# Three attention stages: score products in two row halves, far distance term in the operands, VectorE on the near half only, zero spans left out

## The chip, the core and the metric

One Trainium2 chip, of which the program uses one core. A core has TensorE (PE in the profile; PEld is its weight load), VectorE (DVE), ScalarE (ACT), GpSimd (POOL) and SyncE (SP, which here only issues DMAs). The matrix results lie in PSUM, everything else that the engines touch in SBUF. The metric is the device time of one execution in microseconds, median of several runs.

## What is computed

A block of eight layers over `x` of shape (4, 1024, 128): attention a, a mixture of experts, attention b, the same mixture of experts again, a fast-weights layer, a LoRA layer, attention c and the LoRA layer again. Each takes a layer norm of `x` first. Only the three attentions are touched. They have 16 heads of 8 dimensions, 4 batches and 1024 tokens:

```python
# a: distance term added to the scores
scores = jnp.einsum('bqhd,bkhd->bhqk', q, k) / math.sqrt(head_dim)
bias = -jnp.abs(pos[None, :] - pos[:, None])
scores = scores + slopes[None, :, None, None] * bias[None, None]   # slopes[h] = 0.7071 ** h
probs = jax.nn.softmax(scores, axis=-1)
...
# b: scores multiplied by a distance factor
scores = jnp.einsum('bhsd,bhtd->bhst', q, k) / jnp.sqrt(D)
decay = jnp.exp(-jnp.abs(distance_decay[0]) * dist)
attn = jax.nn.softmax(scores * decay, axis=-1)
...
# c: no distance term, heads centred over the tokens
corr = jax.nn.softmax(jnp.einsum('bthd,bThd->bhtT', x_centered, x_centered), axis=-1)
```

## The kernel before

The eight layers run one after the other, each in its own blocks; the block of one step starts when all engines have left the one before. Every engine has its own instruction stream, and semaphores tie them. The order is written out by hand, so nothing is planned by a tool.

An attention layer is: `layer_norm` (L77; with it POOL clears the operand buffers, `Operands.clear`, L336), `project_qkv` (L189; c has `centre_and_split` in its place), for a and b `bound_scores` and a branch (`choose`, L983) that takes the fast form when a bound on the scores is below a limit, then `attend_transposed` (L623), `normalise` and `project_out`.

`project_qkv` makes q and k in 16 units of 128 features x 512 tokens (w = 0 is q, w = 1 is k). To keep float32 accuracy in bf16 products each number is split into three bf16 parts: DVE adds the bias (L257), ACT casts the first part (L298), DVE takes the rest (L266), ACT casts the second part (L304), POOL makes the third (L311), and SP stores the three parts into `parts_dram` (L319). ACT also squares (L301) for the bound.

`attend_transposed` works on 16 groups, one for four heads (GH = 4) of one batch. The operands of a score product are six combinations of the parts, 8 rows each, so 48 of the 128 rows of PE are in use; the others hold zeros (c has one more row, at 64, with the shift). A group has 32 units: eight blocks J of 128 keys by four heads j. The steps of a unit:

- `scores` (L702 to L716): two products c = 0, 1 of 128 keys x 512 queries into a slot of `s_ps`; there are three slots (SLOTS), and the wait at L709 or L711 is for the slot's last reader.
- in b, DVE multiplies the 1024 scores by a slice of the distance table and writes `probs` in SBUF (L836); in a it does slope x distance + score (L838) for the heads j = 1, 2, 3. ACT then takes the exponential in place (L779). In a the head j = 0 goes another way: ACT takes the exponential from PSUM (L775), and POOL multiplies by a factor table (L694). In c ACT reads the scores straight from PSUM (L786).
- `sum_up` (L718 to L732): per J and half c, four float32 products with `v_cols` (one per head, each in its own 32 columns of PE) add to `o_ps`. It waits for the exponential of the block's last head.

PE's order is fixed in `pair` (L734): the products of unit n + 3, then, at n % 4 = 3 and n % 4 = 1, one half's sums. After a group the sums are copied to `out_t`: by ACT in a and b (`take_sums`, L762, after its second unit of the next group), by DVE in c (L820). The loads of a group's operands (L672, 12 DMAs of 64 KB; L675 in c) are issued by SP into one of two buffers when the sums of the group before last have been taken. The DVE loop runs over head groups and then batches, as do all others.

## Time and profile before

| | us |
|---|---|
| median of three runs | 3812.92 |
| range of the runs | 3808.32 to 3816.82 |
| span of the profiled execution | 3812.1 |
| PE busy in it | 3231.4 (85%) |
| DVE busy | 2548.2 (67%) |
| ACT busy | 2544.1 (67%) |
| POOL busy | 721.3 (19%) |
| first to last start of a score product: a | 562.8 |
| the same, b | 596.1 |
| the same, c | 516.4 |

The three attention loops together are 1675 us of the span, 44%. The shares of busy time over the whole span are averages over layers with different limits, so each stage has to be read by itself. The spans of the matmuls are modelled at their ends: the start times say more than the busy time. The chain that ended last covers only the last layer, since the layers are kept apart by blocks.

### The profile page before, as it was taken

Reading aid. Unit: us, or ns where it says so; the run is one execution under the profiler, and the core shown is the slowest. Engines: PE = TensorE matmul, PEld = TensorE weight load, DVE = VectorE, ACT = ScalarE, POOL = GpSimd, SP = SyncE. Lnnn points to the kernel's source line nnn. Section 1 sums busy time; section 2 is a strip of 40 time slices with the busy share of each in tenths; the row PEclk is TensorE's granted clock in tenths of the full one; section 3 lists DMA queues with packets and bytes.
Section 4 is the critical chain, followed back from the end, with each engine's and each line's share of the span. In section 5 each row is a group of like instructions: output and inputs, shape, how many; then the busy total and the mean of one; then the engine's idle time right before and its main releaser. Section 6 shows DMA issues by size and latency. Waiting matters only on the chain. (4 is left out here: it accounts for less than half of the span.)

```text
span 3812.1 us, 55628 instructions
## 1 busy us (share of the span) xinstructions
PE 3231.4 (85%) x18220; PEld 1431.3 (38%) x18220; DVE 2548.2 (67%) x3577; ACT 2544.1 (67%) x3503; POOL 721.3 (19%) x395
## 2 busy tenths in 40 slices
PE   3899999799996688888889999788878367999987
PEld 2122222567764211111257766522356341222235
DVE  6788888677777699999967777577799551000022
ACT  5899999455444699999845545555433347999971
POOL 4455555000002200000000000165544010000010
PEclk8999999899998899999989999899989558999995
DMA  3111110000000211111000000000000001111100
GB/s 97 30 18 24 25 21 13 23 0 1 0 0 5 84 25 17 25 17 25 9 23 0 1 0 0 24 1 0 0 0 0 2 22 39 25 25 25 25 11 23
DMA packets 47299, 66.97 MB, mean 18 GB/s; under 512 B 6993, under 2 KB 25297, under 8 KB 46545
## 3 DMA queue, kind: packets, MB, share of 16 engines
q1 hardware_dynamic: 47184, 65.54, 8.2%
q8 instruction: 60, 0.98, 0.1%
q14 instruction: 55, 0.44, 0.0%
HBM read 47.56 MB, written 17.96 MB: 17 GB/s over the span
## 5 line engine op out<-in xcount | busy, mean ns | idle before, releaser
L836 DVE TENSOR_TENSOR b_direct_probs<-b_direct_s_ps,b_distance 128x1024 f32<-128x1024 f32 x512 | 583.4, 1212 | 30.4 <-PE b_direct_s_ps L713 16.7
L779 ACT ACTIVATE b_direct_probs<-b_direct_probs 128x1024 f32<-128x1024 f32 x512 | 534.7, 1057 | 74.1 <-DVE b_direct_probs L836 45.2
L838 DVE SCALAR_TENSOR_TENSOR a_direct_probs<-a_distance,a_slopes,a_direct_s_ps 128x1024 f32<-128x1024 f32 x384 | 470.3, 1277 | 111.4 <-PE a_direct_s_ps L713 111.4
L1353 ACT ACTIVATE m_mix_hidden<-m_mix_up_ps 128x512 f32<-128x512 f32 x512 | 305.7, 597 | 295.3 <-PE m_mix_up_ps L1297 295.3
L786 ACT ACTIVATE c_att_probs<-c_att_s_ps 128x1024 f32<-128x1024 f32 x512 | 482.5, 1029 | 13.7 <-PE c_att_o_ps L728 13.1
L1305 PE MATMUL m_mix_down_ps<-m_w,m_mix_hidden 128*128 128x128 f32 x4096 | 474.8, 276 | 0.0
L1305 PEld LDWEIGHTS m_mix_down_ps<-m_w,m_mix_hidden 128*128 128x128 f32 x4096 | 467.2, 192 | 15.3 <-issue 15.3
L1297 PE MATMUL m_mix_up_ps<-m_mix_ZT,m_w 128*128 128x512 f32 x1024 | 471.6, 619 | 0.0
L779 ACT ACTIVATE a_direct_probs<-a_direct_probs 128x1024 f32<-128x1024 f32 x384 | 400.4, 1057 | 36.2 <-DVE a_direct_probs L838 12.5
L820 DVE COPY c_out_t<-c_att_o_ps 128x512 f32 x32 | 20.6, 686 | 515.1 <-PE c_att_o_ps L728 515.1
L694 POOL TENSOR_TENSOR a_direct_probs<-a_direct_probs,a_XN 128x1024 f32<-128x1024 f32 x128 | 304.4, 2379 | 266.7 <-ACT a_direct_probs L775 266.7
L728 PE MATMUL b_direct_o_ps<-b_direct_probs,b_v_cols 128*32 128x512 f32 x2048 | 269.4, 604 | 59.1 <-ACT b_direct_probs L779 59.0
L713 PE MATMUL b_direct_s_ps<-b_q_rows,b_k_rows 128*128 128x512 bf16 x1024 | 277.2, 386 | 37.0 <-DVE b_direct_probs L836 18.6
L713 PE MATMUL c_att_s_ps<-c_q_rows,c_k_rows 128*128 128x512 bf16 x1024 | 271.1, 385 | 43.2 <-DMA c_q_rows<-shift 31.5
L728 PE MATMUL a_direct_o_ps<-a_direct_probs,a_v_cols 128*32 128x512 f32 x2048 | 269.4, 604 | 37.9 <-ACT a_direct_probs L779 28.3
L713 PE MATMUL a_direct_s_ps<-a_q_rows,a_k_rows 128*128 128x512 bf16 x1024 | 270.3, 384 | 32.7 <-DMA a_k_rows<-qk_parts 18.2
L728 PE MATMUL c_att_o_ps<-c_att_probs,c_v_cols 128*32 128x512 f32 x2048 | 269.5, 604 | 0.4 <-ACT c_att_probs L786 0.4
L1297 PEld LDWEIGHTS m_mix_up_ps<-m_mix_ZT,m_w 128*128 128x128 f32 x1024 | 157.4, 190 | 291.1 <-ACT m_mix_hidden L1353 274.1
L1458 DVE TENSOR_REDUCE m_mix_mixed<-m_mix_weighted 128x128 f32<-128x1024 f32 x128 | 246.8, 1928 | 4.4
L1273 POOL TENSOR_TENSOR X<-X,m_Z x16 | 22.0, 1376 | 985.1 <-DVE m_Z L1462 985.1
L713 PEld LDWEIGHTS c_att_s_ps<-c_q_rows,c_k_rows 128*128 128x128 bf16 x1024 | 78.1, 98 | 318.9 <-ACT c_att_probs L786 233.6
L1669 POOL TENSOR_TENSOR f_recur_dots_prods<-f_recur_dots_vecs 128x512 f32<-128x512 f32 (+1 forms) x64 | 173.0, 2715 | 104.2 <-DVE f_recur_dots_vecs L1701 104.2
(330 smaller groups left out, 3982.7 us busy)
## 6 DMA issues: line engine op xcount, KB each, us to landing
qk_parts<-a_qkv_parts SPq DMA_DIRECT2D x16, 384.0 KB, 2.5
a_q_rows<-qk_parts SPq DMA_DIRECT2D x96, 64.0 KB
a_k_rows<-qk_parts SPq DMA_DIRECT2D x96, 64.0 KB
qk_parts<-b_qkv_parts SPq DMA_DIRECT2D x16, 384.0 KB, 2.5
b_q_rows<-qk_parts SPq DMA_DIRECT2D x96, 64.0 KB
b_k_rows<-qk_parts SPq DMA_DIRECT2D x96, 64.0 KB
c_q_rows<-qk_parts SPq DMA_DIRECT2D x96, 64.0 KB
c_k_rows<-qk_parts SPq DMA_DIRECT2D x96, 64.0 KB
```

The costliest lines, as they stand in the source:

```text
L694: pool.tensor_tensor(first, first, factor[:, at:at + SEQ], ALU.mult).then_inc(damped, 1)
L713: last = pe.matmul(s_ps[:, n % SLOTS, c * BANK:(c + 1) * BANK], k_rows[:, half, j, J * P:(J + 1) * P], q_rows[:, half, j, c * BANK:(c + 1) ...
L728: last = pe.matmul(o_ps[VW * j:VW * (j + 1), c, :], v_cols[:, half, J, j, :], probs[:, J % 2, j, c * BANK:(c + 1) * BANK], start=(J == 0), ...
L779: act.activation(out, out, ACT.Exp).then_inc(exped, 1)
L786: act.activation(out, s_ps[:, n % SLOTS, :], ACT.Exp).then_inc(exped, 1)
L836: ins = dve.tensor_tensor(out, scores_, near, ALU.mult)
L838: ins = dve.scalar_tensor_tensor(out=out, in0=near, scalar=slopes[:, bass.ds(hg * GH + j, 1)], in1=scores_, op0=ALU.mult, op1=ALU.add)
L1297: pe.matmul(up_ps[:, f % UP_BANKS, :], w["w1"][:, f * P:(f + 1) * P], ZT[:, half, :], start=True, stop=True).then_inc(up_done, 1)
L1305: last = pe.matmul(down_ps[:, t % 2, e, :], hidden[:, e * HALVES + h, t * P:(t + 1) * P], w["w2"][:, e * HALVES + h, :], start=(h == 0), s ...
L1353: act.activation(hidden[:, f, :], up_ps[:, f % UP_BANKS, :], ACT.Silu).then_inc(silu_done, 1)
L1458: dve.tensor_reduce(mixed[:, :], weighted[:, :, :].rearrange("p e d -> p d e"), AX, ALU.add).then_inc(summed, 1)
L1669: return engine.tensor_tensor(prods[:, c % 2, at:at + n, :], vecs[:, c % 2, 0:n, :], vecs[:, c % 2, other:other + 1, :].to_broadcast([P, n ...
```

## The change

1. **Two row halves.** The 48 operand rows stand twice, at rows 0 to 47 and 64 to 111 (`PAIR_ROW = 64`). The two products of a unit take 64 rows each, one the upper and one the lower half, in place of 128 rows each. SP issues 24 loads a group in place of 12; in c the query rows are half as long each, and one shift row goes to each half.
2. **Near and far.** Of a unit's 1024 queries, the 512 on the side on which its keys lie are near, the others far. For the far side the distance splits into a key's distance to the middle and a query's, so that its term can be put into the operands: in a six more rows with the products of slope x distance (`BiasRows`, made by POOL in the layer norm and stored in `bias_dram`; two more loads a group), in b a second, damped version of q and k (`damp`), which doubles the split and the store in `project_qkv` (16 units, now 32 splits). DVE works only on the near side, in place in PSUM, for all four heads.
3. **ACT from PSUM in all three.** The exponential reads `s_ps` and writes `probs`. A slot is free when ACT has read it, where before it was free when DVE had. The factor table, POOL's product and the ACT copies of the sums are gone; DVE takes the sums, after its third unit of the next group.
4. **Zero spans.** In a `alibi_span` leaves out queries so far from the keys that the exponential is zero: for head h beyond ceil(152 / slope). Widths are 280 to 942 of 1024 for the first four heads (mean 556.1; the near part 433.8), 736 to 1024 for the next four (mean 991.8), full for the rest. Sums over a left-out edge are cut in two pieces.
5. **Loops.** Batches outside, head groups inside and written out; an exponential ahead of the loop (`warm`). `clear` writes the rows of ones only in c, in two stretches of 32 rows. The limit of the branch in a is 24 in place of 30.

```diff
@@ project_qkv
+            def take(x):
+                u, v = divmod(x, VERS)
...
+                if v == 0:
+                    dve.wait_ge(projected, u + 1)
+                    dve.tensor_scalar(full[:, b, :], qk_ps[:, u % RING, :], b_qk[:, w:w + 1],
+                                      scale if w == 0 else 1.0, ALU.add, ALU.mult).then_inc(biased, 1)
+                else:
...
+                    dve.tensor_tensor(full[:, b, :], full[:, (x - 1) % RING, :], damp[:, at:at + CHUNK],
+                                      ALU.mult).then_inc(biased, 1)
@@ attend_transposed
+            def scores(hg, n, b):
...
+                at = hg * UNITS + n
+                back = at - SLOTS if at >= SLOTS else max(m for m in range(-SLOTS, 0) if slot(0, m + NB) == slot(0, at))
+                pe.wait_ge(exped, b * NB + (back + 1 + SLOTS))
                 for c in range(2):
-                    last = pe.matmul(s_ps[:, n % SLOTS, c * BANK:(c + 1) * BANK],
-                                     k_rows[:, half, j, J * P:(J + 1) * P],
-                                     q_rows[:, half, j, c * BANK:(c + 1) * BANK], start=True, stop=True)
+                    if not part(hg * GH + j, J, c):
+                        continue
+                    left, right = part(hg * GH + j, J, c)
+                    tile = int(c != J // (JT // 2)) if by_dve else c
+                    rows = slice(PAIR_ROW * tile, PAIR_ROW * (tile + 1))
+                    last = pe.matmul(s_ps[:, slot(hg, n), left:right], k_rows[rows, half, j, J * P:(J + 1) * P],
+                                     q_rows[rows, half, j, left:right], start=True, stop=True)
                 last.then_inc(scored, 1)
...
+                        act.activation(probs[:, J % 2, j, lo:hi], s_ps[:, slot(hg, n), lo:hi], ACT.Exp).then_inc(exped, 1)
...
+                if slopes is None:
+                    ins = dve.tensor_tensor(held, held, near, ALU.mult)
+                else:
+                    h = hg * GH + j
+                    ins = dve.scalar_tensor_tensor(out=held, in0=near, scalar=slopes[:, h:h + 1], in1=held,
+                                                   op0=ALU.mult, op1=ALU.add)
...
+                    for n in range(UNITS):
+                        adjust(b, hg, n)
+                        if n == SLOTS - 1:
+                            if hg:
+                                take_sums(b, hg - 1)
@@ alibi_attention
+def alibi_span(h, J):
+
+
+    reach = math.ceil((UNDERFLOW + 2 * SAFE_BAND_SCORE) / alibi_slopes()[h])
+    return max(0, J * P - reach), min(SEQ, (J + 1) * P + reach)
```

The copies of the sums change their engine. ACT's stream in b before, at the start of a group inside its loop (L779 is the exponential, L766 the copy; the other rows keep registers):

```order
L779 ACTIVATE b_direct_probs<-b_direct_probs 128x1024
L778 REGISTER_ALU
L779 ACTIVATE b_direct_probs<-b_direct_probs 128x1024
L763 ISA
L766 ISA
L766 COPY b_out_t<-b_direct_o_ps 128x512
L766 ISA
L766 COPY b_out_t<-b_direct_o_ps 128x512
L778 REGISTER_ALU
```

DVE's stream in b now, over the first batch (L828 is the product on the near half, now in place in `s_ps`; L817 the copy of a group's sums):

```order
L828 TENSOR_TENSOR b_direct_s_ps<-b_direct_s_ps,b_distance 128x512 x35
L817 COPY b_out_t<-b_direct_o_ps 128x512 x2
L828 TENSOR_TENSOR b_direct_s_ps<-b_direct_s_ps,b_distance 128x512 x32
L817 COPY b_out_t<-b_direct_o_ps 128x512 x2
L828 TENSOR_TENSOR b_direct_s_ps<-b_direct_s_ps,b_distance 128x512 x32
L817 COPY b_out_t<-b_direct_o_ps 128x512 x2
L828 TENSOR_TENSOR b_direct_s_ps<-b_direct_s_ps,b_distance 128x512 x29
```

The two copies stood behind ACT's second unit and stand behind DVE's third unit of the next group; 32 adjustments lie between two pairs.

In `project_qkv` of b DVE's stream is now, for the units four and five (L262 is the bias, L267 the damping product, L276 the rest, L285 the bias of v):

```order
L262 TENSOR_SCALAR b_qkv_full<-b_qkv_qk_ps,b_b_qk 128x512
L276 TENSOR_TENSOR b_qkv_rest<-b_qkv_full,b_qkv_parts 128x512
L285 TENSOR_TENSOR b_V<-b_qkv_v_ps,b_b_v 128x512
L267 TENSOR_TENSOR b_qkv_full<-b_qkv_full,b_damp 128x512
L276 TENSOR_TENSOR b_qkv_rest<-b_qkv_full,b_qkv_parts 128x512
L262 TENSOR_SCALAR b_qkv_full<-b_qkv_qk_ps,b_b_qk 128x512
L276 TENSOR_TENSOR b_qkv_rest<-b_qkv_full,b_qkv_parts 128x512
```

Where a unit had one bias and one rest, it now has a damping product and a second rest as well.

PE's stream in a now, in the first head group (L741 score products, L760 sums):

```order
L741 MATMUL a_direct_s_ps<-a_q_rows,a_k_rows 128x512
L741 MATMUL a_direct_s_ps<-a_q_rows,a_k_rows 128x48
L748 ISA
L749 ISA
L760 MATMUL a_direct_o_ps<-a_direct_probs,a_v_cols 32x280
L760 MATMUL a_direct_o_ps<-a_direct_probs,a_v_cols 32x343
L760 MATMUL a_direct_o_ps<-a_direct_probs,a_v_cols 32x432
L760 MATMUL a_direct_o_ps<-a_direct_probs,a_v_cols 32x512
```

Every product there was 512 wide; now each is as wide as its head's span.

## Rows read from the trace of the kernel before

**Rows 1.** Groups by line: busy us, mean ns of one, idle before and releaser.

```profile
L836 DVE TENSOR_TENSOR b_direct_probs<-b_direct_s_ps,b_distance 128x1024 f32<-128x1024 f32 x512 | 583.4, 1212 | 30.4 <-PE b_direct_s_ps L713 16.7 <-PE b_direct_o_ps L728 12.5
L838 DVE SCALAR_TENSOR_TENSOR a_direct_probs<-a_distance,a_slopes,a_direct_s_ps 128x1024 f32<-128x1024 f32 x384 | 470.3, 1277 | 111.4 <-PE a_direct_s_ps L713 111.4
L779 ACT ACTIVATE b_direct_probs<-b_direct_probs 128x1024 f32<-128x1024 f32 x512 | 534.7, 1057 | 74.1 <-DVE b_direct_probs L836 45.2
L786 ACT ACTIVATE c_att_probs<-c_att_s_ps 128x1024 f32<-128x1024 f32 x512 | 482.5, 1029 | 13.7 <-PE c_att_o_ps L728 13.1
L1353 ACT ACTIVATE m_mix_hidden<-m_mix_up_ps 128x512 f32<-128x512 f32 x512 | 305.7, 597 | 295.3 <-PE m_mix_up_ps L1297 295.3
L786 ACT ACT_TABLE_LOAD x16 | 20.5, 1283 | 24.2 <-PE c_att_s_ps L713 23.9
```

**Rows 2.** Timeline of c, two half steps: start us, length us, instructions, idle before.

```profile
3312.06 1.04 PE L713 MATMUL c_att_s_ps<-c_q_rows,c_k_rows 128*128 128x512 bf16 x4
3312.19 3.77 ACT L786 ACTIVATE c_att_probs<-c_att_s_ps 128x1024 f32<-128x1024 f32 x4 [0.16 <-PE c_att_o_ps L728]
3313.02 1.07 PE L728 MATMUL c_att_o_ps<-c_att_probs,c_v_cols 128*32 128x512 f32 x8
3314.02 1.04 PE L713 MATMUL c_att_s_ps<-c_q_rows,c_k_rows 128*128 128x512 bf16 x4
```

**Rows 3.** Timeline of b at the end of a group.

```profile
1413.93 1.92 PE L728 MATMUL b_direct_o_ps<-b_direct_probs,b_v_cols 128*32 128x512 f32 x16
```

**Rows 4.** Timeline of c: the copies of a group's sums by DVE.

```profile
3303.15 1.29 DVE L820 COPY c_out_t<-c_att_o_ps 128x512 f32 x2 [30.99 <-PE c_att_o_ps L728]
```

**Rows 5.** Groups by line: DVE products of 128x512.

```profile
L2039 DVE TENSOR_TENSOR X<-X,l_y_ps 128x512 f32<-128x512 f32 x16 | 11.0, 687 | 85.6 <-PE l_y_ps L2005 85.6
L1701 DVE SCALAR_TENSOR_TENSOR f_recur_dots_vecs<-f_recur_dots_vec_ps,f_recur_dots_low 128x512 f32<-128x512 f32 x128 | 85.3, 683 | 71.6 <-ACT f_recur_dots_low L1659 71.1
```

**Rows 6.** Timeline: the first loads of a, and the first score product.

```profile
90.96 3.08 SPq L672 DMA_DIRECT2D a_q_rows<-qk_parts  x6
94.28 2.44 SPq L672 DMA_DIRECT2D a_k_rows<-qk_parts  x6
102.69 0.61 PE L713 MATMUL a_direct_s_ps<-a_q_rows,a_k_rows 128*128 128x512 bf16 x1 [18.18 <-DMA a_k_rows<-qk_parts]
```

**Rows 7.** Stretches: us, busy us of the engines, granted clock, DMA share, GB/s.

```profile
3340.00:3342.00 2.00, 2.00 (x20) 0.47 (x12) 0.00 (x0) 1.98 (x3) 0.00 (x0) 1.00 0.53 79
```

**Rows 8.** Groups by line: DVE in the projection of b.

```profile
L266 DVE TENSOR_TENSOR b_qkv_rest<-b_qkv_full,b_qkv_parts 128x512 f32<-128x512 f32 x16 | 14.3, 893 | 0.7 <-ACT b_qkv_parts L298 0.7
L257 DVE TENSOR_SCALAR b_qkv_full<-b_qkv_qk_ps,b_b_qk 128x512 f32<-128x512 f32 x16 | 11.8, 740 | 11.9 <-PE b_qkv_qk_ps L242 11.9
```

**Rows 9.** Timeline of c's layer norm: POOL clears, DVE normalises.

```profile
3104.21 6.92 POOL L341 MEMSET c_k_rows<- 1x8192 bf16 x1
3104.24 8.57 DVE L112 TENSOR_SCALAR c_XN<-X,c_ln_neg_mean,c_ln_rstd 128x128 f32<-128x128 f32 x8
3114.28 2.14 DVE L112 TENSOR_SCALAR c_XN<-X,c_ln_neg_mean,c_ln_rstd 128x128 f32<-128x128 f32 x8
```

**Rows 10.** Groups by line: POOL's product of 128x1024, in a.

```profile
L694 POOL TENSOR_TENSOR a_direct_probs<-a_direct_probs,a_XN 128x1024 f32<-128x1024 f32 x128 | 304.4, 2379 | 266.7 <-ACT a_direct_probs L775 266.7
```

**Rows 11.** PE stretches with alternating row counts (last layer), and one plain.

```profile
3751.59 0.79 PE L2005 MATMUL l_y_ps<-l_lora_b,l_outer_t 64*128 64x128 f32 x2
3752.31 0.79 PE L2003 MATMUL l_y_ps<-l_lora,l_XT 128*128 128x128 f32 x2
2947.30 3.63 PE L1795 MATMUL f_recur_values_y_ps<-f_out,f_recur_values_mixed_t 128*128 128x128 f32 x16 [1.10 <-ACT f_recur_values_mixed_t L1828]
```

**Rows 12.** Stretches with the granted clock (seventh figure).

```profile
1300.00:1600.00 300.00, 260.85 (x1523) 55.83 (x1524) 291.58 (x256) 273.01 (x270) 2.82 (x7) 0.99 0.13 21
2953.00:2960.00 7.00, 5.04 (x41) 4.62 (x42) 4.15 (x5) 1.01 (x1) 0.00 (x0) 1.00 0.00 0
3750.00:3800.00 50.00, 50.00 (x154) 35.04 (x152) 9.02 (x14) 4.64 (x8) 0.00 (x0) 0.50 0.00 0
```

More of the change, by code:

```diff
@@ L812, in _ @@
+            with act.Fori(0, BATCH) as b:
+                batch(b)
         @block.vector
@@ new lines, in batch @@
+            def batch(b, first):
+                for hg in range(HG):
+                    if not by_dve:
+                        take_sums(b, hg)
+                        continue
+                    for n in range(UNITS):
+                        adjust(b, hg, n)
+                        if n == SLOTS - 1:
+                            if hg:
+                                take_sums(b, hg - 1)
+                            elif not first:
+                                take_sums(b - 1, HG - 1)
```

436 lines of the change are left out of this document (231 added, 205 removed).

## Prediction

> **What bounds the kernel now.** The totals come first and say little: three busy engines over stages with different limits. So I read the groups by line, then the timeline inside each attention loop. In **b** VectorE is the bound: its 512 products of 1212 ns with 30.4 us of idle time are 614 us of the stage, ScalarE has 74.1 us of idle time, most of it for DVE [rows 1]. In **a** DVE has only three heads of four (470.3 us plus 111.4 idle), and POOL's 128 products of 2379 ns form a second chain beside it [rows 1, 10]. In **c** DVE has no product. There TensorE sets the pace: a half step of two units is 1.96 us from one start of products to the next (3312.06 to 3314.02), of which 0.96 are four products and 1.00 the sums; a block J is 3.92 us. ACT's four exponentials take 3.77 us of it and wait 0.16 [rows 2]. The 482.5 us over 512 are 0.942 us of ACT a unit (the single record, 1029 ns, overlaps its neighbour) [rows 1].
>
> **What the change makes of it.** Row halves, near halves and the reading from PSUM leave ACT as the only engine with 0.942 us of work a unit in all three stages: DVE's product of 128x512 takes 0.683 to 0.687 us [rows 5], and PE must fall below 3.77 us a block.
>
> *PE.* Today 8 products of 0.24 us and two sums phases make 3.92 us [rows 2]. If the two halves run side by side, a unit costs one product time: 4 x 0.24 + 2 x 1.00 = 2.96 us, with four more switches of geometry 3.3. That the array can work on separate parts at once, rows 2 show for columns only: eight records of sums (four float32 products) take 1.07 us, though one alone must stream its 512 columns several times. That it does so for rows nothing here shows. Side by side costs 0 against the ACT bound; one after the other leaves 3.92 us or more. I take side by side, since the two halves read other rows, other weights and another PSUM bank each. The Trainium skill, "TensorE: Matmul & The Clock Gate", Part 3: Packing small matmuls, states a measured 3.07 times for four row tiles, and that weight loads overlap only between different row groups; by it this step holds, and no row here can check it.
>
> *The slot chain.* A slot now waits for: end of its exponential, 0.05, the products 0.24 to 0.4, DVE 0.69, 0.05: about 1.2 us. With three slots it has 2 x 0.942 = 1.88 us. A sums phase of 1.00 us in front of the products [rows 2] costs at most the rest of the slack, 0.7. So no wait inside a group.
>
> *The end of a group, a and b.* DVE now takes the sums, after its third product of the next group. Let the last exponential end at T. PE runs the next products and both halves' sums of the last block, 0.41 + 1.92 [rows 3], then 0.17, DVE's two copies, 1.29 [rows 4]: T + 3.8. Only then comes the adjustment of the fourth unit, 0.69: T + 4.5. ACT has three units ready and would want it at T + 2.83. Stall: 1.7 us a group; its cover is those three units. Between 0.5 (PE splits its sums sooner) and 2.5. In c no adjustment is behind the copies: none.
>
> - **b**: 32 x 0.942 = 30.15, + 1.7 = 31.85 a group, x 16 = 509.5, minus 3 for the tail that "first to last start" leaves out: 506.5 against 596.1: **-90**.
> - **c**: 16 x 30.15 - 3 = 480 against 516.4: **-36**. The 16 table loads (20.5 us, [rows 1]) lie in that gain: ACT has one left.
> - **a**: ACT costs 0.844 us per 1000 columns ((1029 - 597) / 512, [rows 1]) plus 0.078 a unit so that 1024 give 0.942. Widths of 991.8 give 0.915: 29.3 + 1.7 = 31.0 for the second head group; the third and fourth 31.85 each. In the first, mean width 556.1, ACT needs 0.547 a unit, 17.5 a group. But there the cover is gone: a block of four units is 2.2 us of ACT and PE's two sums phases alone are near 2. Each phase delays the slot chain; I add 0.55 us to half the units: 17.5 + 8.8 + 1.7 = 28.0. Bounds: 19.2 (all hidden) and 31.85 (no gain at all). Four batches: 4 x (28.0 + 31.0 + 2 x 31.85) = 491, minus 3 = 488 against 562.8: **-75**, bounds -110 and -59. Cutting the first group's sums in pieces adds PE instructions, not columns. POOL leaves the loop; where its chain stood [rows 10], DVE's fourth head stands at 0.69.
>
> *Loads.* SP issues 24 or 26 a group in place of 12. Inside a loop they have the time from T + 3.8 to the end of the next group, 24 to 28 us; 12 took 11.7 us from first issue to use (90.96 to 102.69, [rows 6]), twice that is 23.5: hidden, with nothing to spare in a's first group. Nor does a transfer slow PE: 3340 to 3342 has DMA at 0.53 and a PE that issues as in rows 2 [rows 7]. But the first group of a stage has no cover: its 12 more loads stand in SP's queue ahead of the first product. 12 issues took 5.8 us (rows 6: 3.08 + 2.44 and the gap), 12 loads wholly 11.7; between these +8.5 a stage, **+25** for three (18 to 35).
>
> *Projection of b.* Each of 16 units gets one more product (0.69) and one more rest (0.69 to 0.89, [rows 5, 8]) on DVE, which had 11.9 us idle over the 16 [rows 8]: 1.4 each, **+22** (12 to 30). ACT, POOL and SP get a second split too, but less than DVE in sum.
>
> *Layer norms.* In a, POOL's BiasRows are some 16 short and 8 row-long operations on 1024 elements; a memset of one partition and 8192 took 6.92 [rows 9], and goes. DVE beside a busy POOL took 8.57 us for eight normalisations that took 2.14 without [rows 9]. **+8** for a (2 to 14); **-5** for b (the memset goes, two iotas and one exponential come); **+7** for c (a second memset of 6.92). Sum +10.
>
> Sum: -90 - 36 - 75 + 25 + 22 + 10 = **-144** against the execution's own 3812.1, so 3668; the median of the runs is 0.8 higher: **3669 us**.
>
> **Rivals.**
> *Row halves one after the other.* The block on PE is then 3.92 us plus what b's and a's group ends add: c keeps its 516 (+36), b and the last three head groups of a lose 0.15 to 0.25 us a block (+31 and +23): 3669 + 90 = 3759. For it: no row shows rows in parallel. Against: other banks, other rows.
> *Switches and queues.* PE changes geometry four times a block more often than it would with whole-array products. In the last layer, where products of 64 and 128 rows alternate, one starts every 0.36 x 2 = 0.72 us, while a run of 8 equal ones (16 records) takes 3.63, 0.454 each [rows 11]: 0.27 us a switch at the low clock, perhaps half at the high one. On the 3.3 us block that is up to 0.5 more, 3.8: ACT waits now and then, most in a's first head group. With steady loads that no longer fit, +18 in a, +9 in b, +4 in c at least: 3700 to 3760. The Trainium skill, "TensorEngine Tiling (Array Packing)", Key Properties, says that changing the mode drains the engine; by it this is the likelier direction of error, and rows 11 agree with a cost of 0.27 us.
> *Less than forecast is lost*: the first head group at its floor and group ends nearly hidden, below 3640.
> *Slower: the granted clock.* The change leaves PE with gaps: some 3 of 3.77 us busy. The records show 0.99 in b's loop with PE busy 87% and 1.00 at 5.04 of 7 us, but also 0.50 at 100% busy in the alternating stretch of the last layer, where the rows in use change like here [rows 12]. If the loops were granted 0.5 (1.2 GHz), a block would be about 1.9 + 2 x 2.0 + switches = 6.2 us in place of 3.77: +2.4 x 128 = +310 us a stage. One stage at that clock gives 3980, all three about 4550. It turns the result at 144 / 930, 16% of the attention time.
> *The change doesn't do what it says*: the fast form is left if the bound in a exceeds 24; over the given inputs the longest q times the longest k is 13, so it is taken.
>
> **How the numbers follow.** Forecast 0.65; row halves serial 0.10; switches and queues 0.11; below 3640 0.08; clock 0.04; elsewhere within 0.2% 0.01, slower for a cause not named 0.01. The measurement tells 0.2%, about 8 us, from no change. Faster 0.94, same 0.01, slower 0.05. The forecast's own bounds (stalls -1.2 to +0.8 a group, the first head group -35 to +15, loads -7 to +10, projection -10 to +8) rarely fall together: 3635 to 3700. Half of the two PE rivals has to be within, so the range is 3630 to 3745.
>
> **What would show it.** Right: in c ACT busy with no idle time before L786's successor, unit pace 0.94, pairs of products with one start; in b and a one gap of 1 to 2.5 us a group on ACT, released by DVE, right behind the two copies. First product of a stage some 8 us later after the first load. Granted clock 1.00. Wrong: pairs with starts 0.216 us apart; ACT released by PE inside a group of b or c; SP's loads the last releaser at a group's start; a clock of 0.5 in any loop; the first head group of a at over 30 us.

## The result and the profile after

The changed kernel takes 3771.95 us (median of four runs, 3769.95 to 3773.79) against 3813.69: ratio 0.989, 95% interval 0.9876 to 0.9904. It is faster by 1.1%, as forecast in its direction, but by 42 us instead of 144, and lies outside the range (3630 to 3745). The profiled execution has a span of 3772.1 us against 3812.1.

Where the 40 us of the two profiled executions come from (a loop is counted from the first to the last start of a score product, and the stretches between the loops):

| us | before | after | change | forecast |
|---|---|---|---|---|
| loop of a | 562.8 | 550.8 | -12 | -75 |
| loop of b | 596.1 | 516.1 | -80 | -90 |
| loop of c | 516.4 | 472.0 | -44 | -36 |
| first load of a stage to its first product (a, b, c) | 11.7, 10.9, 11.5 | 28.6, 27.2, 19.6 | +41 | +25 |
| projection of b, first bias to last rest | 32.9 | 69.2 | +36 | +22 |
| layer norms, the rest | | | +19 | +10 |

The large miss is a's loop, the next two are the first loads and b's projection. The page's groups, line, out<-in, count | busy, mean ns of one | idle before and what ended it, show that ACT reads PSUM everywhere and where it waits:

```profile
L804 ACT ACTIVATE a_direct_probs<-a_direct_s_ps 128x1024 f32<-128x1024 f32 (+10 forms) x512 | 432.5, 939 | 148.6 <-DVE a_direct_s_ps L831 111.4
L804 ACT ACTIVATE b_direct_probs<-b_direct_s_ps 128x1024 f32<-128x1024 f32 x512 | 474.8, 1092 | 71.6 <-DVE b_direct_s_ps L828 63.9
L804 ACT ACTIVATE c_att_probs<-c_att_s_ps 128x1024 f32<-128x1024 f32 x512 | 470.2, 1166 | 22.5 <-PE c_att_s_ps L741 19.5
L828 DVE TENSOR_TENSOR b_direct_s_ps<-b_direct_s_ps,b_distance 128x512 f32<-128x512 f32 x512 | 333.6, 695 | 181.5 <-PE b_direct_s_ps L741 181.4
```

Beside [rows 1]: DVE has 181.5 us of idle time in b instead of 30.4, and is no longer the bound. ACT is busy for 0.918 us a unit in c (470.2 / 512), a little less than the 0.942 that PE had set. In a, though, ACT has 148.6 us of idle time.

**c and the inside of a group went as forecast.** The timeline of c after (start us, length us), beside [rows 2]:

```profile
3312.04 1.07 PE L760 MATMUL c_att_o_ps<-c_att_probs,c_v_cols 128*32 128x512 f32 x8
3313.04 0.91 PE L741 MATMUL c_att_s_ps<-c_q_rows,c_k_rows 64*128 64x512 bf16 x4
3313.88 1.06 PE L760 MATMUL c_att_o_ps<-c_att_probs,c_v_cols 128*32 128x512 f32 x8
3314.87 0.91 PE L741 MATMUL c_att_s_ps<-c_q_rows,c_k_rows 64*128 64x512 bf16 x4
```

Two units take 1.83 us instead of 1.96, and the pace is now ACT's. A pair of 64-row products has one start (3 ns apart in the records), where the 128-row products before stood 226 ns apart, so the two row halves do run side by side. The Trainium skill, "TensorE: Matmul & The Clock Gate", Part 3: Packing small matmuls, has products on different rows of the array run at the same time, and the trace agrees.

**The end of a group in b** (timeline) is the stall that the prediction worked out:

```profile
1562.74 1.92 PE L760 MATMUL b_direct_o_ps<-b_direct_probs,b_v_cols 128*32 128x512 f32 x16
1564.60 0.96 PE L741 MATMUL b_direct_s_ps<-b_q_rows,b_k_rows 64*128 64x512 bf16 x6
1564.86 1.29 DVE L817 COPY b_out_t<-b_direct_o_ps 128x512 f32 x2 [1.23 <-PE b_direct_o_ps L760]
1566.07 1.89 DVE L828 TENSOR_TENSOR b_direct_s_ps<-b_direct_s_ps,b_distance 128x512 f32<-128x512 f32 x3
1566.80 23.94 ACT L804 ACTIVATE b_direct_probs<-b_direct_s_ps 128x1024 f32<-128x1024 f32 x26 [1.68 <-DVE b_direct_s_ps L828]
```

Both halves' sums, two copies, then the adjustment, and ACT resumes after 1.68 us (1.9 in the mean over b's groups); 1.7 was forecast. Behind it ACT runs 26 exponentials without a gap.

**The loads** are what the prediction had too cheap. First the timeline at the start of a: first and last issue of the first group's 26 loads and the first product, then the stretch of 28 us and, for comparison, 2 us of the first group's loads in the kernel before (us, busy us of PE, PEld, DVE, ACT, POOL, granted clock, DMA share, GB/s):

```profile
97.00 0.40 SPq L697 DMA_DIRECT2D a_k_rows<-qk_parts  x1
...
107.00 0.29 SPq L712 DMA_DIRECT2D a_k_rows<-bias_rows  x1
...
125.64 1.05 PE L741 MATMUL a_direct_s_ps<-a_q_rows,a_k_rows 64*128 64x280 bf16 x3 [34.61 <-DMA a_k_rows<-bias_rows]
```

```profile
97.00:125.00 28.00, 0.00 (x0) 0.00 (x0) 0.00 (x0) 0.61 (x2) 0.71 (x2) 0.50 0.52 67
```

```profile
98.00:100.00 2.00, 0.00 (x0) 0.00 (x0) 0.00 (x0) 0.00 (x0) 0.00 (x0) 0.50 0.55 83
```

All 26 are issued in 10 us, but land 18.6 us after the last issue. The DMA share stands at 0.52 all the while, with nothing else to load: of the 16 DMA engines' time half is used, and between 102 and 120 us the trace has never fewer than 8 packets in flight and mostly 8. The share was the same before. But the loads have become slower too: 67 GB/s in place of some 83, and a packet of 2 KB takes 251 ns in the mean where it took 185. In half_loads below, with 14 loads, it is 247 ns, so the number of loads is not the reason; what is, stays open. The same holds inside the loop. The loads for a's third group, and that group's start (timeline):

```profile
158.86 0.29 SPq L697 DMA_DIRECT2D a_k_rows<-qk_parts  x1
...
187.76 0.61 PE L741 MATMUL a_direct_s_ps<-a_q_rows,a_k_rows 64*128 64x512 bf16 x2 [3.75 <-DMA a_k_rows<-bias_rows]
...
190.31 1.02 ACT L804 ACTIVATE a_direct_probs<-a_direct_s_ps 128x1024 f32<-128x1024 f32 x1 [4.43 <-PE a_direct_o_ps L760]
```

28.9 us again from the first issue to the use, and PE stands 3.75 us for it, with ACT behind. The waits of a's loop (engine, what it waited for: us in total, times, longest) say how often:

```profile
PE a_direct_s_ps L741 <- DMA a_k_rows<-bias_rows: 65.7, 13, 34.6
```

34.6 of this is the start of the stage; 31 us are the starts of twelve groups. And the clock (stretches of the three loops, granted clock the third figure from the end), beside 1.00, 1.00 and 0.99 of the same stretches before:

```profile
125.60:677.00 551.40, 455.78 (x3132) 112.02 (x3136) 371.67 (x542) 430.76 (x511) 5.63 (x14) 0.88 0.36 46
1367.00:1884.00 517.00, 444.99 (x3056) 89.07 (x3056) 351.55 (x542) 473.39 (x511) 5.63 (x14) 0.96 0.36 46
3170.70:3643.00 472.30, 432.74 (x3048) 89.04 (x3048) 19.33 (x30) 468.13 (x511) 5.64 (x14) 0.99 0.27 38
```

In a PE was granted half the clock (1.2 GHz) for 130 us of the loop, before the change for 5. That time is twice what the granted clock lacks to 1, times the stretch: 2 x 0.118 x 551.

### The profile page after: what moved, and what is told of

It is laid out like the page before. It is cut to its first block and busy times, and to the rows that moved or that the text cites. A ratio compares the mean times of both kernels' runs of the same rounds, so it can differ in the third digit from the quotient of the medians.

```text
span 3772.1 us, 56220 instructions
## 1 busy us (share of the span) xinstructions
PE 3041.1 (81%) x18300; PEld 1382.0 (37%) x18300; DVE 2266.9 (60%) x3801; ACT 2361.2 (63%) x3456; POOL 452.0 (12%) x310
## 5 line engine op out<-in xcount | busy, mean ns | idle before, releaser
L804 ACT ACTIVATE a_direct_probs<-a_direct_s_ps 128x1024 f32<-128x1024 f32 (+10 forms) x512 | 432.5, 939 | 148.6 <-DVE a_direct_s_ps L831 111.4
L804 ACT ACTIVATE b_direct_probs<-b_direct_s_ps 128x1024 f32<-128x1024 f32 x512 | 474.8, 1092 | 71.6 <-DVE b_direct_s_ps L828 63.9
L804 ACT ACTIVATE c_att_probs<-c_att_s_ps 128x1024 f32<-128x1024 f32 x512 | 470.2, 1166 | 22.5 <-PE c_att_s_ps L741 19.5
L831 DVE SCALAR_TENSOR_TENSOR a_direct_s_ps<-a_distance,a_slopes,a_direct_s_ps 128x512 f32<-128x512 f32 (+3 forms) x512 | 354.1, 732 | 195.2 <-PE a_direct_s_ps L741 194.1
L828 DVE TENSOR_TENSOR b_direct_s_ps<-b_direct_s_ps,b_distance 128x512 f32<-128x512 f32 x512 | 333.6, 695 | 181.5 <-PE b_direct_s_ps L741 181.4
L817 DVE COPY c_out_t<-c_att_o_ps 128x512 f32 x32 | 20.6, 686 | 479.1 <-PE c_att_o_ps L760 479.1
L741 PE MATMUL a_direct_s_ps<-a_q_rows,a_k_rows 64*128 64x512 bf16 (+12 forms) x984 | 201.3, 400 | 130.2 <-DMA a_k_rows<-bias_rows 65.7
L760 PE MATMUL a_direct_o_ps<-a_direct_probs,a_v_cols 128*32 128x512 f32 (+14 forms) x2168 | 289.9, 592 | 1.0 <-ACT a_direct_probs L804 1.0
L741 PE MATMUL b_direct_s_ps<-b_q_rows,b_k_rows 64*128 64x512 bf16 x1024 | 199.8, 402 | 103.7 <-ACT b_direct_probs L804 39.8
L760 PE MATMUL b_direct_o_ps<-b_direct_probs,b_v_cols 128*32 128x512 f32 x2048 | 280.1, 625 | 2.3 <-ACT b_direct_probs L804 2.3
L760 PE MATMUL c_att_o_ps<-c_att_probs,c_v_cols 128*32 128x512 f32 x2048 | 271.2, 607 | 1.0 <-ACT c_att_probs L804 1.0
L741 PE MATMUL c_att_s_ps<-c_q_rows,c_k_rows 64*128 64x512 bf16 x1024 | 197.4, 390 | 78.7 <-DMA c_q_rows<-shift 39.2
L741 PEld LDWEIGHTS b_direct_s_ps<-b_q_rows,b_k_rows 64*128 64x128 bf16 x1024 | 47.0, 93 | 387.7 <-ACT b_direct_probs L804 339.7
L741 PEld LDWEIGHTS a_direct_s_ps<-a_q_rows,a_k_rows 64*128 64x128 bf16 x984 | 45.9, 95 | 376.5 <-ACT a_direct_probs L804 287.1
L741 PEld LDWEIGHTS c_att_s_ps<-c_q_rows,c_k_rows 64*128 64x128 bf16 x1024 | 47.6, 93 | 358.7 <-ACT c_att_probs L804 315.2
```

The costliest lines, as they stand in the source:

```text
L741: last = pe.matmul(s_ps[:, slot(hg, n), left:right], k_rows[rows, half, j, J * P:(J + 1) * P], q_rows[rows, half, j, left:right], start=Tr ...
L760: last = pe.matmul(o_ps[VW * j:VW * (j + 1), c, lo - c * BANK:hi - c * BANK], v_cols[:, hg % 2, J, j, :], probs[:, J % 2, j, lo:hi], start ...
L804: act.activation(probs[:, J % 2, j, lo:hi], s_ps[:, slot(hg, n), lo:hi], ACT.Exp).then_inc(exped, 1)
L828: ins = dve.tensor_tensor(held, held, near, ALU.mult)
L831: ins = dve.scalar_tensor_tensor(out=held, in0=near, scalar=slopes[:, h:h + 1], in1=held, op0=ALU.mult, op1=ALU.add)
```

## The experiments

Theory A: the doubled loads bound a's groups and the start of every stage, because they use only half of the DMA engines, and the low clock in a follows largely from these waits. Theory B: PE's gaps and its geometry switches inside the loop cost the time. The names of the kernels are those of the table. Each kernel below is the changed kernel with one edit unless it says otherwise. The loops of all of them (first to last start of a score product) follow. a's loop is the same code and the same loads in the changed kernel, damp_psum and no_damp, and takes 551, 555 and 564 us: that much it varies from one execution to another, so differences of a's loop below some 13 us prove nothing by themselves.

| kernel | median us | a | b | c | us at half clock in a, b, c |
|---|---|---|---|---|---|
| before | 3814 | 562.8 | 596.1 | 516.4 | 5, 5, 8 |
| changed | 3772 | 550.8 | 516.1 | 472.0 | 130, 46, 10 |
| half_loads | 3679 | 497.8 | 509.8 | 471.7 | 60, 31, 9 |
| pool_sem | 3705 | 499.5 | 511.2 | 471.1 | 67, 36, 8 |
| full_spans | 3781 | 564.6 | 519.6 | 471.0 | 105, 44, 7 |
| pool_full | 3709 | 505.5 | 510.4 | 471.1 | 27, 38, 8 |
| serial_rows | 4330 | 780.1 | 811.1 | 532.3 | 595, 610, 61 |
| rows128 | 3770 | 528.1 | 540.7 | 506.3 | 25, 6, 4 |
| rows64 | 4300 | 794.1 | 860.9 | 531.9 | 644, 721, 60 |
| damp_psum | 3761 | 554.5 | 516.1 | 470.9 | 134, 51, 7 |
| no_damp | 3744 | 564.1 | 517.5 | 473.0 | 120, 49, 8 |
| split_sums | 3766 | 558.8 | 509.0 | 471.1 | 106, 34, 8 |
| all3 | 3657 | 476.6 | 498.2 | 471.1 | 25, 28, 8 |

Three expectations below use 140 us of half clock for a's loop in the changed kernel and 605 for serial_rows; 130 and 595 are right. No conclusion hangs on the difference.

### Half of the loads left out

```
-        LOADS = 4 * len(Q_PARTS) + 2 * (bias_dram is not None or shift_dram is not None)
+        LOADS = 2 * len(Q_PARTS) + 2 * (bias_dram is not None) + (shift_dram is not None)
...
-                    for tile in range(2):
+                    for tile in range(1):
```

> The changed kernel, all three attentions without the loads of rows 64 to 111 (the second copy of the operands; those rows hold zeros, so one half of the scores is without its product; a keeps its two loads of bias rows, c one shift row). Same work on PE, DVE and ACT, 12 to 14 loads a group in place of 24 to 26. In the changed kernel's trace the first product of a waits 28.6 us from the first issue, c and b likewise, and a's groups begin 2.6 to 3.5 us late. Theory A, the loads are the bound of a and the start of every stage, and the low clock of a comes from PE's idle time at the group starts: first products some 14, 13 and 9 us after the first issue, -13 in a and b each and -6 in c; a's groups fall from 34.5 to about 32 (the first head group to 28), -45; stretches at clock 0.5 in a's loop fall from 140 us to under 50. In all 3772 - 32 - 45 - up to 15 = 3680 to 3695. Theory B, PE's gaps and geometry switches inside the loop cost the time and the clock: only the starts move, 3740, and 0.5 stands in a for over 100 us as before.

3679.25 us (two runs), 93 less. The stages start 11, 13 and 10 us sooner (the stretch before each loop), a's loop loses 53 us and b's 6. The waits of a's loop for loads are the stage's start alone:

```profile
PE a_direct_s_ps L741 <- DMA a_k_rows<-bias_rows: 22.8, 1, 22.8
```

The time at half clock in a falls by more than half (130 to 60 us, where theory A had under 50). Theory A holds, theory B's 3740 does not. PE and DVE run the same instructions in both kernels, so the clock's fall in a is to that extent the loads' doing, unless the zeros in half of the rows have a part in it; the next kernel has the real operands. Of the 53 us, 31 are the waits themselves; that the other 22 are products and sums at half clock is argued, not separated, and 13 of them lie within what a's loop varies.

### The second half's loads issued by POOL

```
-        loaded = [k.sem(f"{tag}_loaded{half}") for half in range(2)]
+        loaded_sp = [k.sem(f"{tag}_loaded{half}") for half in range(2)]
+        loaded_pool = [k.sem(f"{tag}_pooled{half}") for half in range(2)]
...
+        def load(eng, b, hg, tile):
+            loaded = (loaded_sp, loaded_pool)[tile]
...
+                    load(sp, b, hg, 0)
...
+                    load(pool, b, hg, 1)
```

> The changed kernel, with the loads of the second row half issued by POOL with a semaphore of their own; same bytes, same result. While a group's 26 loads run, the DMA share of the changed kernel stands at 0.5 and 8 packets are in flight. Theory A, the loads are bound by the DMA engines that SP's queue uses for this shape, and POOL's queue uses others too: as fast as without the second half's loads (3679), 3675 to 3700, with a's loop near 505 and DMA share above 0.5 at a stage's start. Theory C, the limit is that of the shape whoever issues: no change, 3765 to 3780, or slower by POOL's own cost of issuing, up to +20.

3705.22 us, ratio 0.9715 to before (0.9699 to 0.9731), with the same bytes and the same result. a's loop is 499.5, as with half of the loads, none of its group starts waits, and it has 67 us at half clock, so the zeros of half_loads were not what kept the clock up. Theory A holds and theory C's 3765 to 3780 does not. The profiled execution (span 3692.3) lies 17 us above that of half_loads (3675.0), 5 of them at the start of a and 8 ahead of c, where the stage starts keep a part of the price. The other three runs took 3704 to 3707, and the median is a little over the expected 3700; no trace shows why they are longer than the profiled one. The stretch at the start of a, first of this kernel, then of the changed one:

```profile
97.00:107.00 10.00, 0.00 (x0) 0.00 (x0) 0.00 (x0) 0.07 (x1) 9.18 (x17) 0.50 0.80 104
```

```profile
97.00:107.00 10.00, 0.00 (x0) 0.00 (x0) 0.00 (x0) 0.61 (x2) 0.71 (x2) 0.50 0.48 67
```

The same shape of load from two issuers has a DMA share of 0.80 and 104 GB/s, from one 0.48 and 67; the 26 loads take 23.2 us (96.4 to 119.6) instead of 28.6. So what held SP's loads of 8 partitions at half is not a limit of the shape whoever issues. The Trainium skill, "DMA: Bandwidth & Descriptors", Why a DMA increments its semaphore by 16 and not by 1, says that a transfer runs on the largest number up to 16 that divides both outermost dimensions, for SP's queue always the lowest-numbered ones, for POOL's from a cursor that moves on; by it an 8-partition load takes 8, and the traces agree: 8 packets in flight and a share of 0.5. That POOL's loads gained because they ran on other engines is the page's reading; no run here tells it from a limit of SP's queue. I had not weighed that rule.

### Full spans in a, with SP's loads and with POOL's

```
-                                      slopes=slopes, bias_dram=bias_dram, span=alibi_span)
+                                      slopes=slopes, bias_dram=bias_dram)
```

> The changed kernel with full spans in a: the first two head groups compute all 1024 queries of each unit. Theory A, a's groups are bound by their 26 loads (about 28.6 us from issue to landing, plus 4 to 5 us from the group's start to the issue), whatever ACT has to do: a's loop stays at 552 within 12 us, 3765 to 3785. Rival: the narrow spans save what ACT's widths say, 11 to 14 us a batch for the first head group and 1 for the second, so leaving them out costs 45 to 60, 3820.

> The kernel of pool_sem with full spans in a. With SP's loads, full spans cost 9 us (3781 against 3772), since a's groups were bound by their loads. Theory A: with the loads no longer the bound, the spans' worth shows: the first head group goes from 30.3 us to the 32.0 to 33.5 of the others, the second from 30.5 to 31.1: 4 x 3 = +12, up to +16 with the widths of ACT's floor: 3717 to 3722. The forecast for the change had put the first head group at 28.0 against 31.85, 15 us. Rival, the spans are worth nothing or even cost since PE is the bound there in either form: 3700 to 3706.

3781.37 with SP's loads, 9 us more than the changed kernel, in theory A's interval: the part of the change that leaves work out was worth little while loads bound the groups. 3709.01 with POOL's, 4 us more than pool_sem (two runs, 3706.28 and 3711.75, against 3694.03 to 3706.76): no difference that can be told. Here theory A's 3717 to 3722 fell, and the rival's 3700 to 3706 is the nearer one. The first head group averages 30.3 us a group in pool_sem with narrow spans and 30.9 with full ones in pool_full, since with short exponentials ACT is no longer what is late there: a block of four units still has PE's two sums phases, at half clock in part (67 us of a's loop at half clock with narrow spans, 50 of them in the four groups of the first head group; 27 and 16 with full spans). So the zero spans leave out two fifths of ACT's work in a quarter of a's groups (17.5 us of 30.15 remain) and return nothing that can be measured in this form.

### Both products on the same 64 rows

```
-                    rows = slice(PAIR_ROW * tile, PAIR_ROW * (tile + 1))
+                    rows = slice(0, PAIR_ROW)
```

> The changed kernel with both products of a unit on rows 0 to 63 (the second half's rows are loaded and not used, so a and b lack the far side's distance term). Theory A, two row halves run side by side and this is what c gained from: pairs start 0.216 us apart, c's block of four units goes from 3.67 to 3.9 us or more, c's loop from 473 to about 510; b's groups from 32.2 to about 34, +28; a, bound by its loads, by 0 to 15. In all 3835 to 3850. Rival: the pairs gain nothing that counts, c's gain came from something else (the table loads, the loop order): c within 5 us, 3772.

4330.38 us, ratio 1.1355 (1.1207 to 1.1503). Both theories missed by 480 us or more: c stayed within 25 us (532 against 510, its first group at half clock), a and b stood at half clock for some 600 us each (its loops of a and b):

```profile
124.30:905.00 780.70, 739.59 (x3132) 159.90 (x3136) 383.71 (x542) 452.55 (x511) 5.61 (x14) 0.62 0.26 33
1594.00:2406.00 812.00, 785.29 (x3052) 140.66 (x3054) 365.98 (x541) 503.10 (x511) 5.61 (x14) 0.62 0.24 30
```

PE is busy for 95% and 97% of these stretches, more than in the changed kernel, and is granted less. So the clock can fall without PE having less to do. Groups of the same loop take 34 to 36 us at full and 55 to 60 at half clock.

### One product after the other, on 128 rows and on 64

Both kernels leave out the second half's loads and the bias rows (so that part of the scores' terms is missing), and differ in one line. This is rows128; rows64 has `slice(0, PAIR_ROW)` there.

```
-                    rows = slice(PAIR_ROW * tile, PAIR_ROW * (tile + 1))
+                    rows = slice(0, P)
```

> The kernel of half_loads (no loads of rows 64 to 111) also without a's bias rows, with each product of a unit on all 128 rows instead of its 64, one after the other as in the kernel before. With both products on the same 64 rows the clock stood at 0.5 for 605 us of a's loop and 610 of b's, and the run took 4330. If it is the rows in use that decide (128 rows in turn keep the clock as they did before): clock 1.0 after the first group, c's groups 32.3 as before the change against 29.4, b's 34 against 31.1, a's 33 against 31: 3679 + 46 + 46 + 30 = 3800, 3775 to 3820. If it is only that PE has more to do in a block than ACT (any serial form falls to the low clock): 4200 and more, with 0.5 in a and b.

> The kernel of rows128 (half the loads, no bias rows, products one after the other) with each product on rows 0 to 63 instead of all 128: the same number of products, columns, waits and loads, only the rows in use differ. serial_rows differed from rows128 in the loads too, whose waits at the group starts could be what sends the clock down. Theory F, the rows in use decide whether the clock stays up: clock 0.5 for most of a's and b's loops as in serial_rows (605 and 610 us of them), 4150 to 4330. Rival, the load waits started the fall in serial_rows and there are none here: clock near 1.0 as in rows128, 3765 to 3800.

3769.51 us with 128 rows, about 4300 with 64 (two runs, 4215.56 at a mean granted clock of 0.81 and 4383.61 at 0.77; the profile is of the second). Theory F holds, its rival's 3765 to 3800 does not. The loops of a and b, rows128 first, then rows64:

```profile
112.80:641.00 528.20, 475.50 (x3072) 122.06 (x3128) 370.62 (x541) 443.69 (x511) 5.60 (x14) 0.98 0.18 23
1319.00:1860.00 541.00, 502.37 (x2994) 104.05 (x3046) 350.51 (x541) 493.19 (x511) 5.61 (x14) 0.99 0.17 23
```

```profile
110.80:905.00 794.20, 760.94 (x3128) 163.95 (x3128) 384.01 (x541) 453.51 (x511) 5.60 (x14) 0.59 0.12 15
1583.00:2445.00 862.00, 836.01 (x3048) 147.67 (x3048) 368.61 (x541) 504.30 (x511) 5.60 (x14) 0.58 0.11 14
```

The same instructions, columns and loads; with half of the rows in use the clock falls and stays low. Load waits are not needed for it. Nor is it the data: the rows that rows128 adds hold zeros. The two timelines of b, at full clock with 128 rows, at half clock with 64:

```profile
1500.38 1.04 PE L737 MATMUL b_direct_s_ps<-b_q_rows,b_k_rows 128*128 128x512 bf16 x4
1501.35 1.06 PE L756 MATMUL b_direct_o_ps<-b_direct_probs,b_v_cols 128*32 128x512 f32 x8
1502.35 1.09 PE L737 MATMUL b_direct_s_ps<-b_q_rows,b_k_rows 128*128 128x512 bf16 x4
```

```profile
1852.63 1.88 PE L737 MATMUL b_direct_s_ps<-b_q_rows,b_k_rows 64*128 64x512 bf16 x4
1854.44 1.93 PE L756 MATMUL b_direct_o_ps<-b_direct_probs,b_v_cols 128*32 128x512 f32 x8
1856.31 1.88 PE L737 MATMUL b_direct_s_ps<-b_q_rows,b_k_rows 64*128 64x512 bf16 x4
```

Two units take 1.97 us, or 3.68. In the second PE has no gap at all and is not granted more. rows128 also gives the price of the row halves that serial_rows could not: c's loop 506.3 against 471.7 in half_loads, so that side by side is worth 35 us there, 31 in b (540.7 against 509.8) and 30 in a, though half_loads has the low clock for longer; the forecast's rival had 36, 31 and 23. The rest of c's gain (516.4 to 506.3) is not separated; the table loads are the likeliest part.

### The damped copy of b

Two kernels: one takes it from PSUM (first diff; with it PE waits for both versions before it writes the PSUM buffer again, and the table is scaled once), the other does without it (second, the far half's factor is left out).

```
-                    dve.tensor_tensor(full[:, b, :], full[:, (x - 1) % RING, :], damp[:, at:at + CHUNK],
-                                      ALU.mult).then_inc(biased, 1)
+                    dve.scalar_tensor_tensor(out=full[:, b, :], in0=qk_ps[:, u % RING, :], scalar=b_qk[:, w:w + 1],
+                                             in1=damp[:, at:at + CHUNK], op0=ALU.add, op1=ALU.mult
+                                             ).then_inc(biased, 1)
```

```
-                        count, make_table, SAFE_SCORE, damp[:, :])
+                        count, make_table, SAFE_SCORE)
```

> The changed kernel, with the damped copy of q and k in b's projection taken from PSUM (one scalar_tensor_tensor on qk_ps with the bias and the table, the table scaled once by 8 to the power -1/4) instead of from the SBUF copy. In the trace the SBUF product takes 1340 ns in the median against 674 at least, and the products that read PSUM never more than 751. Theory D, DVE and POOL get in each other's way where both work on SBUF alone: each of the 16 products falls to about 0.75, -8 to -10 us, 3762 to 3765. Rival, the POOL operation beside it only moves its delay to the next DVE operation: the rests get longer by as much, 3770 to 3774.

> The changed kernel without the damped copy in b (neither made, split nor stored; the far half reads the undamped parts, so its distance factor is left out). From the first bias to the last rest the projection took 32 us before the change and 68.5 after. If its second version costs what DVE's two operations and POOL's interference add, that stretch falls back to about 32: -36, 3736, 3732 to 3742. If part of it is hidden or given back by the table work ahead of it, -22 as the forecast had it: 3750.

Without it 3743.62 us, 28 less; the stretch between the loops of a and b falls by 40 us, of which a's loop (564.1 against 550.8) takes 13 back. That stretch is the projection's price: +36 to +40, not +22. From PSUM 3761.28 us (3755.43 to 3766.37), 11 less, a little more than expected. DVE's groups of b's projection, in the changed kernel and in damp_psum:

```profile
L276 DVE TENSOR_TENSOR b_qkv_rest<-b_qkv_full,b_qkv_parts 128x512 f32<-128x512 f32 x32 | 36.0, 1128 | 0.0
L267 DVE TENSOR_TENSOR b_qkv_full<-b_qkv_full,b_damp 128x512 f32<-128x512 f32 x16 | 20.0, 1251 | 0.0
```

```profile
L276 DVE TENSOR_TENSOR b_qkv_rest<-b_qkv_full,b_qkv_parts 128x512 f32<-128x512 f32 x32 | 26.6, 831 | 5.2 <-ACT b_qkv_parts L312 5.1
L266 DVE SCALAR_TENSOR_TENSOR b_qkv_full<-b_qkv_qk_ps,b_b_qk,b_damp 128x512 f32<-128x512 f32 x16 | 11.8, 739 | 0.0
```

The product falls from 1251 to 739 ns, and the rests do not get longer, they fall too, from 1128 to 831. The rival (the delay only moves) is out. In the changed kernel the product meets POOL's third part (timeline; the first product comes before POOL has started, the second beside it):

```profile
1259.27 0.69 DVE L267 TENSOR_TENSOR b_qkv_full<-b_qkv_full,b_damp 128x512 f32<-128x512 f32 x1
...
1261.53 1.35 POOL L326 TENSOR_TENSOR b_qkv_parts<-b_qkv_rest,b_qkv_parts 128x512 bf16<-128x512 f32 x1 [32.60 <-ACT b_qkv_parts L319]
1261.79 1.65 DVE L267 TENSOR_TENSOR b_qkv_full<-b_qkv_full,b_damp 128x512 f32<-128x512 f32 x1
```

1.65 us for what takes 0.69 alone. The Trainium skill, "SBUF — State Buffer", SBUF: two separate sides, says that a DVE operation with two SBUF inputs and a POOL operation that reads SBUF take turns on one pair of ports; the operation with one input in PSUM does not, and the rows agree: from PSUM the 13 products that overlap a POOL operation take 735 to 745 ns, the other three 735 to 743.

### The end of a group in finer steps

```
@@ batch, PE
...
+                                if hg + 1 < HG:
+                                    scores(hg + 1, SLOTS, b)
+                                elif not final:
+                                    scores(0, SLOTS, b + 1)
                                 sum_up(hg, n // GH, 1, b)
...
@@ batch, DVE
-                        if n == SLOTS - 1:
+                        if n in (SLOTS - 1, SLOTS):
                             if hg:
-                                take_sums(b, hg - 1)
+                                take_sums(b, hg - 1, (n - SLOTS + 1,))
```

> The changed kernel, with the end of a group in finer steps: PE issues the next group's fourth product between the two halves' sums, and DVE takes the first half's sums after its third product and the second half's after its fourth. In the trace ACT waits 1.8 us in each of b's 16 groups behind the two copies. Theory E, that wait is PE's and DVE's order alone: sums of one half 0.96, copy 0.65, so the fourth product is adjusted at the last exponential + 2.9 where ACT wants it at 2.83; the wait falls to 0.2 to 0.8 us, -1.2 x 16 = -20 in b; in a, whose groups are bound by the loads, the issue moves earlier by about 0, so 0 to -10: 3742 to 3755. Rival, the wait comes back one unit later: 3768 to 3773.

3765.84 us (3761.04 to 3769.09), 6 less: neither theory's number. b's loop lost 7 us, and a's took 8 more (no more than it varies). From ACT's third exponential of a group to its fourth, b has 2.8 us in the mean in the changed kernel and 1.3 here, and to the fifth 0.9 and 1.7, so the wait fell from 1.9 to 1.1 us; but the waits for loads rose (b's loop, then a's):

```profile
PE b_direct_s_ps L742 <- DMA b_q_rows<-qk_parts: 45.7, 10, 30.3
```

```profile
PE a_direct_s_ps L742 <- DMA a_k_rows<-bias_rows: 101.6, 15, 34.4
```

b's group starts now wait nine times where they had waited three, a's waited 67 us in all instead of 31. What one wait gave back went into the other, since the loads start at the second copy of the sums, which stands a unit later in DVE's order now, and must be in by the end of a group that got shorter.

### The three edits together

> The changed kernel with the three edits together: POOL issues the second row half's loads, b's damped copy comes from PSUM, the end of a group is split in finer steps. Alone they gave 3705, 3761 and 3766 against 3772. In the run with split sums alone the wait behind the copies fell from 1.8 to about 0.9 us in all, but b's groups then waited 1.3 us for their loads and a's 4 to 6 us. Theory E, that gain was real and hidden by the loads: with the loads out of the way it shows, b's and a's groups 0.9 us shorter each, -25 to -30: 3705 - 11 - 27 = 3667, 3655 to 3675. Rival, the gain is lost elsewhere: 3694, the first two edits alone.

3657.3 us, ratio 0.9582 to before (0.9569 to 0.9595), 115 us below the changed kernel and computing the same. pool_sem and damp_psum alone would be about 3694 (3705 less 11; the two were not run together), so the finer steps give some 37 us here where they gave 6 with the loads in the way. The loops say the same: against pool_sem a's is 23 us shorter and b's 13. Theory E is right, and the gain larger than the 27 expected. a's time at half clock falls as well, from 67 to 25 us; what part of the 23 us that is, was not separated. In b's loop the only wait for loads is the stage's first:

```profile
PE b_direct_s_ps L748 <- DMA b_q_rows<-qk_parts: 28.0, 1, 28.0
```

One cost came with the change and has no run. With all three edits b's groups take 30 to 31 us, but the first groups of the second and third batch 35.8 and 38.4. In the latter PE stands still for 5 us, from the 6th to the 11th of the group, without a releaser that the profile shows (timeline, PE alone), and the clock is at half for 10 us around it:

```profile
1532.88 0.61 PE L748 MATMUL b_direct_s_ps<-b_q_rows,b_k_rows 64*128 64x512 bf16 x1 [5.00 <-issue]
```

The same two groups of the changed kernel take 34.8 and 34.3 us, where b's mean is 32.3; the kernel before has no such step (37.4 us for all groups of b but the first). The batch loop with its four groups written out is new at this place; that it is the cause is not shown.

## Why the prediction was wrong

- **Loads, inside the loop: the step that failed.** The prediction put this term at nothing: "12 took 11.7 us ... twice that is 23.5: hidden", within a cover of 24 to 28 us. In the runs the loads of a's groups take 28.6 to 28.9 us from the first issue to the use: there are 26 of them, and each costs 1.10 us where the 12 before had cost 0.98. The issue comes 4 to 5 us into a group, so a group of a cannot be shorter than some 33 us; they took 34.5 in the mean, where 28.0 to 31.85 was forecast. half_loads puts the price at 53 us in a, 6 in b, 0 in c. The hint was there: [rows 7] has a DMA share of 0.53 with a group's loads under way, and I read it as "does not slow PE" instead of "is at its limit".
- **Loads, at a stage's start.** Same cause. I took 8.5 us a stage for 12 more loads, a value between the issue (5.8 us) and the whole (11.7). In a and b it was more than the whole, +16.9 and +16.3; c, +8.1, met the 8.5 by luck, since its query loads are half as long. So bytes, not issues, set it.
- **b's projection: a term too small.** 1.4 us a unit was the count of DVE's operations; the 48 products with both operands in SBUF now mostly meet a POOL operation, and take 1128 to 1251 ns in the mean where 690 to 890 was put: +36 instead of +22.
- **a's first head group.** Forecast at 28.0, and 33.7 in the changed kernel, 30.3 in pool_sem, once the loads are out of the way: PE, not ACT, is late there, partly at half clock. The forecast said that this group has no cover left, but still took what leaving out columns is worth from ACT's widths, and pool_full shows nothing of it. With all three edits the group averages 28.5 us, and 26.6 the one time that it ran wholly at full clock: the 28.0 was near for a kernel that this one was not.
- **The clock.** The slower rival had the right effect, and its reason, gaps on PE, at best in part. The clock fell in a (0.88 over the loop), largely by load waits: without them it is 0.93 to 0.94. But gaps are not needed: with PE 96% busy it stays low in rows64. Its place in the forecast was a chance of 0.04 for a whole stage; a mild form belonged to the likeliest case, as soon as PE stands still between groups.
- **What held.** Row halves side by side (30 to 35 us a stage; the rival of serial rows is out by rows128), ACT as the bound at 0.92 us a unit (0.942 forecast), the stall of 1.7 us a group in b, no wait inside a group in c and none in b at full clock, c's loop within 8 us, b's within 10, the layer norms' sum in sign and rough size (15 us of the 19 in the table's last line, +10 forecast; b's own came out at about +5 instead of -5). Geometry switches cost nothing that shows behind ACT: c's half step with them is 1.83 us.
- **The signs.** Two of the forecast's signs of being wrong came out, both by the step that failed: SP's loads as the last releaser at a's group starts, and a's first head group over 30 us.

## What to carry to other kernels

When a change doubles transfers, work out first at which rate the queue moves this very shape: a DMA share that stayed at 0.5 while only loads ran was a full queue here and not spare room, and a second issuer of another kind raised it. Before a wait is shortened, ask what starts from the same event, since the time may only move to it: the finer group end gave 6 us with the loads behind it and 37 without. Keep two-input SBUF operations of DVE away from a busy POOL by reading one operand from PSUM.

## What the runs showed that I had not expected

- Products one after the other on 64 of 128 rows, beside the same sums, take the granted clock to half and hold it there with PE busy without a gap: 0.59 and 0.58 over two loops, against 0.98 and 0.99 with all 128 rows in use. In c, where no DVE operation stands between product and exponential, the same kernel came back to full clock after the first groups (60 us at half). Pairs on both row halves kept 0.88 to 0.99 in every loop. What in PE's stream decides this is not settled.
- 26 loads (24 of 8 partitions and 64 KB, 2 of 48 KB) take 28.6 us from one issuer at a DMA share of 0.5, and with 12 of them from POOL 23.2 us at up to 0.8.
- A DVE product with both operands in SBUF took up to 1.65 us beside a POOL operation, 0.69 without, and 0.74 with one operand in PSUM whether POOL was busy or not.
